# The opening of a gated cross-attention kernel in another order: dense bf16 run, mask as a selection matrix, Wq by column blocks, K and V spread by loads

## The reference, cut to what matters

```
q = (layernorm(x) @ Wq).reshape(B, N, 16, 32)
k = (context @ Wk).reshape(B, 77, 16, 32)
v = (context @ Wv).reshape(B, 77, 16, 32)
scores = where(mask, q . k * 32 ** -0.5, -max)
x = x + tanh(g_xattn) * (softmax(scores) @ v) @ Wo
x = x + tanh(g_ffn) * ffn(layernorm(x))      # fake-quantised gate, up, down; silu(gate) * up
```

## Time and profile before

| | |
|---|---|
| median of three runs | 667.89 us (667.67 to 668.32) |
| the profiled execution, its own time | 665.65 us |
| its span, first to last instruction | 663.9 us |
| PE / VectorE / ScalarE / GpSimd busy | 96% / 76% / 50% / 25% of the span |
| scores of tile 0 begin (slot 0) | 35.3 us after the span's start |

### The profile page before, as it was taken

The page is one execution under the profiler, slowest core; times in us unless marked ns, Lnnn a source line. Parts: engine busy times, 40 slices in busy tenths (PEclk is TensorE's granted clock), DMA queues, the critical chain, the costliest instruction groups (busy, mean ns, idle before and its releaser), DMA issues. The chain is left out here.

```text
span 663.9 us, 12956 instructions
## 1 busy us (share of the span) xinstructions
PE 634.2 (96%) x4035; PEld 479.8 (72%) x4035; DVE 507.3 (76%) x947; ACT 331.9 (50%) x511; POOL 166.5 (25%) x374
## 2 busy tenths in 40 slices
PE   6888999999999999999999997999999999899997
PEld 6578999999999999999999995444444444344443
DVE  4687878878787878877776755799888888866664
ACT  1455454545444554544443442677555554355553
POOL 5122231323232232211110111110111110047775
PEclk9999999999999999999999998999999999999999
DMA  6259311101102010100000001434765110089623
GB/s 224 95 160 305 94 48 25 48 24 40 31 25 47 24 47 24 33 1 1 1 2 1 1 1 41 150 142 81 207 207 197 24 32 17 0 308 395 273 110 117
DMA packets 49687, 59.83 MB, mean 90 GB/s; under 512 B 32084, under 2 KB 32238, under 8 KB 49646
## 3 DMA queue, kind: packets, MB, share of 16 engines
q1 hardware_dynamic: 43854, 42.52, 21.4%
q10 hardware_dynamic: 5792, 16.80, 7.1%
HBM read 32.50 MB, written 19.92 MB: 79 GB/s over the span
## 5 line engine op out<-in xcount | busy, mean ns | idle before, releaser
L523 DVE TENSOR_REDUCE sb_smax<-ps_s 128x8 f32<-128x616 f32 x64 | 51.1, 798 | 64.1 <-PE ps_s L760 63.9
L1161 PE MATMUL ps_g<-sb_xqT,sb_wgu 128*128 128x512 bf16 x352 | 90.3, 379 | 0.6 <-DVE sb_xqT L1129 0.5
L1161 PE MATMUL ps_u<-sb_xqT,sb_wgu 128*128 128x512 bf16 x352 | 90.3, 379 | 0.0
L1046 ACT ACTIVATE sb_silu<-ps_g,sb_sgu 128x512 f32<-128x512 f32 x88 | 60.5, 687 | 59.1 <-PE ps_g L1161 31.9
L429 ACT COPY sb_pT<-ps_p 128x512 f32<-128x512 f32 (+1 forms) x96 | 46.4, 521 | 70.1 <-PE ps_p L771 70.1
L721 PE MATMUL ps_q<-sb_xT_hi,sb_wq_hi 128*128 128x256 f32 x256 | 77.6, 303 | 2.0 <-DVE sb_q_lo L514 1.5
L782 PE MATMUL ps_o<-sb_vblk,sb_pT 128*128 (+4 forms) x640 | 79.0, 270 | 0.1
L1332 PE MATMUL ps_z<-sb_wdT,sb_hq 128*128 128x512 bf16 x352 | 76.1, 379 | 1.2 <-ACT sb_hq L1259 1.2
L782 PEld LDWEIGHTS ps_o<-sb_vblk,sb_pT 128*128 128x128 f32 (+1 forms) x640 | 76.8, 191 | 0.6 <-ACT sb_pT L429 0.3
L1118 DVE SCALAR_TENSOR_TENSOR sb_h<-ps_u,sb_sgu,sb_silu 128x512 f32<-128x512 f32 (+1 forms) x88 | 65.9, 749 | 14.8 <-PE ps_u L1161 13.7
L723 PE MATMUL ps_q<-sb_xT_hi,sb_wq_lo 128*128 128x256 f32 x256 | 72.3, 282 | 0.0
(11 more groups left out here) (156 smaller groups left out, 1350.3 us busy)
## 6 DMA issues: line engine op xcount, KB each, us to landing
h_spill<-sb_h SPq DMA_DIRECT2D x4, 2816.0 KB, 9.5
sb_h<-h_spill ACTq DMA_DIRECT2D x16, 704.0 KB, 6.2
out_dram<-sb_wgu SPq DMA_DIRECT2D x32, 256.0 KB, 2.0
sb_x<-in_x_dram ACTq DMA_DIRECT2D x1, 4096.0 KB, 17.8
sb_w_in<-in_L_ffn_w_gate_dram SPq DMA_DIRECT2D x11, 256.0 KB, 2.7
sb_w_in<-in_L_ffn_w_up_dram SPq DMA_DIRECT2D x11, 256.0 KB, 2.6
sb_h<-in_L_ffn_w_down_dram SPq DMA_DIRECT2D x4, 704.0 KB, 5.9
sb_x<-in_x_dram SPq DMA_DIRECT2D x2, 1024.0 KB, 12.2
```

The source lines that it names most:

```text
L523: dve.tensor_reduce(smax[:, half, :].rearrange("p (g h) -> p g h", g=2), half_scores(), X, ALU.max).then_inc(v_max, 1)
L1046: act.activation(silu[(j * KI + i) % 2][:, :, :].rearrange("p t n -> p (t n)"), p_g[(j * KI + i) % 2][:, :], ACT.Silu, scale=sgu[:, i:i + ...
L1161: last = pe.matmul(banks[(j * KI + i) % 2][:, :], wgu[:, what, k, i * P:(i + 1) * P], xqT[j][:, k, :], start=(k == 0), stop=(k == KD - 1))
```

## The change

The result stays the same function. Loads: `x` tiles 0 and 1 now go first, tiles 2 and 3 ahead of `Wk` and `Wq`, and tiles 8 to 11 come right behind tiles 4 to 7. The mask and the four scalars are loaded to one partition and spread by a product with a row of ones. The masked context is no longer worked out elementwise: VectorE builds a small matrix `pickw` (77 x 77 for each batch), and TensorE multiplies the context by it. The 24 float32 products of the identity become nine bf16 products of 512 columns at the start and two more ahead of the keys. `Wq` is split into high and low parts in four column blocks, each with a wait of its own. The keys leave PSUM by one copy (`kc_hi`) and one subtraction (`kc_lo`), and eight loads on SyncE spread them over `k_hi` and `k_lo`. The values of batch 0 are spread as before but alone; those of batch 1 are made in slot 0 and spread by two groups of six loads between the loads of the feed-forward weights. `wo_hi` moves from slot 1 to slot 0, `wo_lo` from slot 2 to slot 1.

```diff
...
+kc_hi, kc_lo = [spare[:, (5 + 4 * i) * B * M:(9 + 4 * i) * B * M].bitcast(F32R)
+                .rearrange("p (b g m) -> p b g m", b=B, g=KD) for i in range(2)]
+small = spare[:, 13 * B * M:]
 rank, none = small[:, 0:B], small[:, B:2 * B]
-keepT = small[0:M, 2 * B:3 * B]
-c_0 = small[:, 3 * B:(3 + KC) * B].rearrange("p (k b) -> p k b", k=KC)
-mask_u = small[:, P:2 * P].bitcast(U8)[:, 0:B * M].rearrange("p (b m) -> p b m", b=B)
-maskT_u = small[0:M, 2 * P:3 * P].bitcast(U8)[:, 0:B]
-v_sb = pT[0:M, :, :].rearrange("p a n -> p (a n)")[:, 0:B * H * VW]\
-    .rearrange("p (b h d) -> p b h d", b=B, h=H)
+keepT, firstT, rankT, kept = [small[0:M, (2 + i) * B:(3 + i) * B] for i in range(4)]
+rampT_i, rampT = small[:, 6 * B:6 * B + 1].bitcast(I32), small[:, 6 * B + 1:6 * B + 2]
+gate_row = small[0:1, 8 * B:8 * B + 4]
+ones_row = small[0:1, P:2 * P]
+mask_row = small[0:1, 2 * P:2 * P + B * M]
+mask_u = small[0:1, 4 * P:5 * P].bitcast(U8)[:, 0:B * M]
+assert H * VW <= 5 * B * M
+v_sb = [a[0:M, 0:H * VW].rearrange("p (h d) -> p h d", h=H)
+        for a in (pT[:, :, :].rearrange("p a n -> p (a n)"), spare)]
...
+    sp.dma_start(x1[:, 0:2, :], x_v[:, 0:2, :]).then_inc(l_x[0], 16)
     sp.dma_start(c_sb, ctx_in.rearrange("b m c -> m b c")).then_inc(l_ctx, 16)
-    sp.dma_start(x1[:, 0:2, :], x_v[:, 0:2, :]).then_inc(l_x[0], 16)
+    sp.dma_start(x1[:, 2:4, :], x_v[:, 2:4, :]).then_inc(l_x[1], 16)
     sp.dma_start(wk_raw, weights(Wk)).then_inc(l_wk, 16)
     sp.dma_start(wq_raw, weights(Wq)).then_inc(l_wq, 16)
-    sp.dma_start(x1[:, 2:4, :], x_v[:, 2:4, :]).then_inc(l_x[1], 16)
     sp.dma_start(wv_raw, weights(Wv)).then_inc(l_wv, 16)
     sp.dma_start(x1[:, 4:8, :], x_v[:, 4:8, :]).then_inc(l_x[2], 16)
+    sp.dma_start(x1[:, 8:12, :], x_v[:, 8:12, :]).then_inc(l_x[3], 16)
     rows(0)
...
-    sp.wait_ge(v_v, 2 * B)
-    sp.wait_ge(g_zero, 9)
-    for k in range(KB):
-        head0, head1 = heads_of(k)
-        for h in range(head0, head1 + 1):
+    sp.wait_ge(g_zero, 8)
+    for kc, k_blk, done in ((kc_hi, k_hi, a_khi), (kc_lo, k_lo, v_klo)):
+        sp.wait_ge(done, 1)
+        for j in range(HG):
+            rows_j = slice(HD * j, HD * j + HD)
+            sp.dma_start(k_blk[rows_j, :, :, M * j:M * j + M].bitcast(F32).rearrange("p b g m -> p (b g) m"),
+                         kc[rows_j, :, :, :].bitcast(F32).rearrange("p b g m -> p (b g) m")).then_inc(l_k, 16)
+
+    spread = [(k, h) for k in range(KB) for h in range(heads_of(k)[0], heads_of(k)[1] + 1)]
+
+    def values_spread(b, part):
+        sp.wait_ge(v_v, 2 * b + 2)
+        for k, h in part:
             r0, r1 = max(P * k, M * h), min(P * k + P, M * h + M, HW)
-            sp.dma_start(vblk[r0 - P * k:r1 - P * k, :, :, SLOT0[k] + h - head0, :],
-                         v_sb[r0 - M * h:r1 - M * h, :, h:H:HH, :]).then_inc(l_v, 16)
+            sp.dma_start(vblk[r0 - P * k:r1 - P * k, b, :, SLOT0[k] + h - heads_of(k)[0], :],
+                         v_sb[b][r0 - M * h:r1 - M * h, h:H:HH, :]).then_inc(l_v[b], 16)
+
+    sp.dma_start(wo_raw, weights(Wo)).then_inc(l_wo, 16)
+    values_spread(0, spread)
     rows(1)
-    sp.dma_start(wo_raw, weights(Wo)).then_inc(l_wo, 16)
-    sp.dma_start(x1[:, 8:12, :], x_v[:, 8:12, :]).then_inc(l_x[3], 16)
-    rows_transposed(0)
     for w in range(2, NW):
+        rows_transposed(w - 2)
         rows(w)
-        rows_transposed(w - 1)
+        if w in (2, 3):
+            values_spread(1, spread[(w - 2) * len(spread) // 2:(w - 1) * len(spread) // 2])
+        if w == KI:
+            sp.wait_ge(l_k, 16 * 2 * HG)
+            sp.wait_ge(l_v[1], 16 * SLOT0[KB])
+    rows_transposed(NW - 2)
...
-    pool.memset(eps[:, :], EPS).then_inc(g_zero, 1)
     pool.memset(minus[:, :], -1.0).then_inc(g_zero, 1)
     pool.memset(step[:, :], 1.0 / QMAX).then_inc(g_zero, 1)
+    pool.wait_ge(g_ramp, 3)
+    pool.tensor_copy(ramp[:, :, :], ramp_i[:, :, :]).then_inc(g_ramp, 1)
+    pool.tensor_copy(rampT, rampT_i).then_inc(g_ramp, 1)
     pool.memset(k_hi[:, :, :, :].bitcast(F32), 0.0).then_inc(g_zero, 1)
+    pool.wait_ge(g_zero, 6)
+    for n in range(4):
+        deviation(n, n)
     pool.memset(k_lo[:, :, :, :].bitcast(F32), 0.0).then_inc(g_zero, 1)
     pool.memset(vblk[:, :, :, :, :], 0.0).then_inc(g_zero, 1)
-    pool.wait_ge(g_zero, 9)
-    for n in range(5):
-        deviation(n, n)
+    deviation(4, 4)
...
-        if isinstance(n, int) and n == 1:
+        if isinstance(n, int) and n == 0:
             act.wait_ge(l_wo, 16)
             act.copy(wo_hi[:, :, :], wo_raw).then_inc(a_wo, 1)
-
+        if isinstance(n, int) and n == 1:
             act.wait_ge(t_v, B)
-            act.wait_ge(v_wq, 1)
+            act.wait_ge(v_wq, KD)
...
-    act.dma_start(mask_u[:, :, :], mask.rearrange("(a b) m -> a b m", a=1)
-                  .broadcast_to([P, B, M])).then_inc(l_mask, 16)
-    for b in range(B):
-        act.dma_start(maskT_u[:, b:b + 1], mask[b:b + 1, :].rearrange("b m -> m b"))\
-           .then_inc(l_maskT, 16)
+    act.dma_start(mask_u, mask.rearrange("(a b) m -> a (b m)", a=1)).then_inc(l_mask, 16)
     for i, a in enumerate((g_xattn, g_ffn, clip_x, clip_down)):
-        act.dma_start(gates[:, i:i + 1], bcast(a)).then_inc(l_small, 16)
+        act.dma_start(gate_row[:, i:i + 1], a.rearrange("(a n) -> a n", a=1)).then_inc(l_small, 16)
+    act.wait_ge(g_zero, 2)
+    act.activation(sg_e[:, 0:1], eps[:, :], ACT.Exp).then_inc(a_dummy, 1)
...
+    def weights_part(g):
+        cols = slice(g * P, (g + 1) * P)
+        act.copy(wq_hi[:, :, cols], wq_raw[:, :, cols]).then_inc(a_wq, 1)
+
     normalise(0, 0)
     x_part(0, 0)
-    normalise(1, 1)
+    act.wait_ge(g_nb, 2)
...
     act.wait_ge(l_wq, 16)
-    act.copy(wq_hi[:, :, :], wq_raw).then_inc(a_wq, 1)
-    x_part(1, 1)
-    act.wait_ge(l_small, 64)
-    act.activation(tg[:, :], gates[:, 0:2], ACT.Tanh).then_inc(a_tg, 1)
-    act.activation(sg_e[:, :], gates[:, 2:4], ACT.Exp, scale=-1.0).then_inc(a_tg, 1)
+    weights_part(0)
+    weights_part(1)
+    x_part(2, 2)
+    weights_part(2)
+    weights_part(3)
     act.wait_ge(t_k, 2)
-    act.wait_ge(g_zero, 7)
-    for j in range(HG):
-        for i in range(2):
-            act.copy(k_hi[HD * j:HD * j + HD, :, 2 * i:2 * i + 2, M * j:M * j + M],
-                     p_k[HD * j:HD * j + HD, i, :, 0:B * M]
-                     .rearrange("p g (b m) -> p b g m", b=B)).then_inc(a_khi, 1)
+    act.copy(kc_hi.rearrange("p b (i g) m -> p i g b m", i=2),
+             p_k[:, :, :, 0:B * M].rearrange("p i g (b m) -> p i g b m", b=B)).then_inc(a_khi, 1)
+    normalise(3, 3)
+    act.wait_ge(t_gate, 1)
+    act.wait_ge(a_dummy, 1)
+    act.activation(tg[:, :], p_gate[:, 0:2], ACT.Tanh).then_inc(a_tg, 1)
+    act.activation(sg_e[:, :], p_gate[:, 2:4], ACT.Exp, scale=-1.0).then_inc(a_tg, 1)
     q_part(0, 0)
-    normalise(2, 2)
-    q_part(1, 1)
-    x_part(2, 2)
-    normalise(3, 3)
     x_part(3, 3)
     normalise(4, 4)
+    q_part(1, 1)
...
+    def values(b):
+        dve.wait_ge(t_v, b + 1)
+        dve.tensor_scalar(v_sb[b][:, :, 0:HD], p_v[b][0:M, :].rearrange("p (h d) -> p h d", h=H),
+                          tg[0:M, 0:1], keepT[:, b:b + 1], ALU.mult, ALU.mult).then_inc(v_v, 1)
+        dve.tensor_copy(v_sb[b][:, :, HD], keepT[:, b:b + 1].broadcast_to([M, H])).then_inc(v_v, 1)
...
+            values(1)
+            dve.wait_ge(v_v, 2 * B)
+            dve.memset(p_p[1][:, 0, :], 0.0).then_inc(v_zero, 1)
...
-        if isinstance(n, int) and n == 2:
+        if isinstance(n, int) and n == 1:
             dve.wait_ge(a_wo, 1)
...
-    dve.wait_ge(t_c, 1)
-    dve.tensor_copy(cT, p_c).then_inc(v_c, 1)
...
-    dve.tensor_tensor(cK, cT, by_chunk(keep), ALU.mult).then_inc(v_mask, 1)
...
-    dve.tensor_tensor(cK, cK, pick, ALU.add).then_inc(v_ck, 1)
...
+    dve.wait_ge(v_mask, 11)
+    for b in range(B):
+        dve.scalar_tensor_tensor(pickw[0:M, b, :], drop[0:M, b, :], firstT[:, b:b + 1],
+                                 pickw[0:M, b, :], ALU.mult, ALU.add).then_inc(v_pick, 1)
+    def query_weights(g):
+        cols = slice(g * P, (g + 1) * P)
+        dve.wait_ge(a_wq, g + 1)
+        dve.tensor_tensor(wq_lo[:, :, cols], wq_raw[:, :, cols], wq_hi[:, :, cols].bitcast(F32),
+                          ALU.subtract).then_inc(v_wq, 1)
...
+    dve.wait_ge(t_ck, 1)
+    dve.tensor_copy(cK, p_ck).then_inc(v_ck, 1)
+    dve.wait_ge(a_xhi, 2)
+    dve.tensor_tensor(xT_lo[0][:, :, P:2 * P], p_x1, xT_hi[0][:, :, P:2 * P].bitcast(F32),
+                      ALU.subtract).then_inc(v_xlo, 1)
+    query_weights(0)
+    query_weights(1)
     x_part(2, 2)
+    query_weights(2)
+    query_weights(3)
+    dve.wait_ge(a_khi, 1)
+    dve.tensor_tensor(kc_lo.rearrange("p b (i g) m -> p i g b m", i=2),
+                      p_k[:, :, :, 0:B * M].rearrange("p i g (b m) -> p i g b m", b=B),
+                      kc_hi.bitcast(F32).rearrange("p b (i g) m -> p i g b m", i=2),
+                      ALU.subtract).then_inc(v_klo, 1)
```

(84 more changed lines are left out.)

123 lines of the change are left out of this document (56 added, 67 removed).

## The result

| | before | after |
|---|---|---|
| median of the runs | 667.75 us (665.30 to 668.58, 10 runs) | 660.32 us (658.60 to 664.70, 10 runs) |
| profiled execution, its own time | 665.65 us | 660.23 us |
| its span | 663.9 us | 658.4 us |
| scores of tile 0 begin | 35.30 us | 26.11 us |

The ratio is 0.9904, 95% interval 0.9883 to 0.9925: faster by some 1%. The forecast was 665.8 us with a range of 663.3 to 669.3 us. In the later comparisons the kernel before had medians of 665.55 to 665.67 us (13 to 29 runs each), against which 660.32 us is 0.8% less: its runs fall in two groups, near 665.5 and near 668 us, and every ratio is taken over such a mix and is not the quotient of the two medians. So beside each ratio I give where a mechanism can be seen without that mix, in the trace.

A forecast was written before the change was run, and what follows sets the result against it. TensorE, busy in 96% of the span, was taken as the bound, with gain only ahead of slot 0: -4.8 us there, +2.7 us in slots 0 to 3, so 667.9 - 2.1 = 665.8 us, range 663.3 to 669.3 us.

The forecast's parts named there:

- Now the same bytes stand ahead of the end of `Wq`: Opening loads: same bytes in another order, so `Wq` lands at 17.4 us and `Wk` at 14 us.
- loads come sooner: Rival, opening: without hundreds of tiny packets `Wq` lands 1.3 us earlier, giving 664.5 us; chance 0.15.
- The keys therefore start at some 14.4 us, as before: Opening: the landing of `Wk` covers the new mask path and dense run, which cost nothing.
- PE's line from the first block: Opening: from `Wq`'s first block at 18.5 us, queries, transposes and values take 11.7 us, ending at 30.2 us.
- The line through the key loads: Opening: `kc_hi` at 20.5 us, eight SyncE issues of 1.0 us, landing 2.0 us; PE's wait ends at 30.5 us.
- (a): Slot 0: VectorE scales batch 1's values, less a saved wait for `xT_lo`: net +0.5 us, bounds 0 and 1.1.
- (b): `wo_hi` stands in front of the copies of `pT`: +1.4 us for PE in slot 1, bounds 0 and 1.9.
- (c): Slot 1: `wo_lo` stands ahead of `q_lo` of tile 3 and `xT_lo` of tile 5: +1.9 us, bounds 0.8 and 2.3.
- (d): Slot 2: the wait for `wo_lo` goes, -1.1 us.
- late key loads: Rival, opening: key loads wait behind others or cost 1.25 us each; slot 0 at 32.5 us, no gain; chance 0.13.
- The clock rival: Opening: gaps after the dense run leave the keys at half clock, +3.3 us, 669.1 us; chance 0.12.
- SyncE as the bound: Rival, opening: each key load takes 1.97 us to issue; keys there at 38.3 us, total 673.6 us; chance 0.10.

The follow-up runs named there:

- e1_wide: Changed kernel with the seven wide mask and scalar loads of before issued again on ScalarE's queue, into unused space: 668.43 us, ratio to the kernel before 1.0039.
- e6_late: Kernel before with the transposed mask and four scalars issued behind the first normalisation on ScalarE: 668.62 us, ratio 1.0037.
- e13_warm16: Kernel before with 16 identity products ahead of the keys in place of 24: 666.12 us, ratio 0.9995.
- e4_whole: Changed kernel with the first tile's queries waiting for all four column blocks of `Wq`: 661.18 us, ratio to the kernel before 0.9926.
- e3_wo: Changed kernel with `wo_hi` back in slot 1 and `wo_lo` back in slot 2: 658.19 us, ratio to the kernel before 0.9875.
- e12_vlate: `e8_halves` with the values of batch 1 moved behind VectorE's first score work of slot 0: 657.02 us, ratio to the kernel before 0.9860.
- e11_stats: Kernel before with VectorE's statistics of `x` tiles 0 and 1 moved ahead of the rest of the mask's chain: 667.96 us, ratio 1.0024.
- e15_both: `e14_xfirst` with the four scalars' loads issued behind the copies of the keys: 665.36 us, ratio to the kernel before 0.9987.
- e5_nodense: Changed kernel without its eleven dense bf16 products: 666.05 us, ratio to the kernel before 0.9984.
- e14_xfirst: `e11_stats` with TensorE's transpose of `x` tile 0 moved ahead of the keys: 666.33 us, ratio to the kernel before 1.0002.
- e2_order: Changed kernel with its first five loads in the order of before: 666.50 us, ratio to the kernel before 1.0007.
- e7_kcopies: Changed kernel with K put in place by the sixteen copies and subtractions of before, no key loads: 663.01 us, ratio to the kernel before 0.9943.
- e8_halves: `e3_wo` with `wo_lo` made in two halves in slot 2, the first earlier in the slot: 656.61 us, ratio to the kernel before 0.9861.

## Why the prediction was wrong, step by step

**What bounds.** "From the steady slots there is nothing to gain" held: -9.2 us lie ahead of slot 0 and +3.5 us in slots 0 to 3.

**"Now the same bytes stand ahead of the end of `Wq`... so `Wq` lands at 17.4 us, and `Wk`... at 14 us"** is the step that failed. It took the rate of the loads from the kernel before, where it was 90 to 108 GB/s from 2 to 6 us, and never asked for the cause of that rate, though the 1.97 us issue was in hand. `Wq` landed at 13.3 us and `Wk` at 10.6 us; `e1_wide` (`Wq` at 16.9 us) and `e6_late` (12.4 us, where the kernel before had 16.1) show that the small loads on ScalarE's queue made the difference. The rival "loads come sooner" named the mechanism but priced it at 1.3 us, with a chance of 0.15; it measured 4.1 us against the 17.4.

Both landings had to be wrong for the miss. The working had two lines to the queries of tile 0 that ended together: the first block of `Wq` at 18.5 us, and the keys, from 14.4 us, through at 18.3 us. With `Wq` alone sooner the queries would have begun at 18.3. They began at 15.09 us because the keys were sooner too, and it was the end of the keys that let them go, not the block.

**"The keys therefore start at some 14.4 us, as before"** failed by 2.8 us, with the landing of `Wk` that stood under it. What the working said for that case came true: with the cover of `Wk` gone the mask path was the start of the chain (`cK` copied at 11.44 us, keys at 11.61). I had also not asked what held the keys at 14.34 us before. It was neither `Wk` (11.9 us) nor `cK` (12.75 us) but the 24 identity products, by `e13_warm16`.

**PE's line from the first block** was nearly right in length: 11.7 us forecast, 26.11 - 15.09 = 11.0 us measured. It began 3.4 us sooner than the 18.5 us forecast. The block split measured 1.6 us (`e4_whole`, with the reserve made there).

**The line through the key loads.** `kc_hi` was due at 20.5 and was done at 16.57 us. I took 1.0 us per issue; eight took 5.38 us with their gaps, 0.67 each, at the cheap end of my bounds. I took 2.0 us for the landing; it was 4.4 and 3.6 us in the median, 3.6 for the last. The two errors cancel in part: from `kc_hi` to the last landing at 25.04 us it was 8.5 us, where I had 10.0, and PE, at slot 0 from 26.11 us, never waited for the loads. By the Trainium skill (DMA: Bandwidth & Descriptors, Specifications), whose 0.6 us to the first byte I had set beside it, the landing would have been further off still.

**Slots 0 to 3.** (a) +0.5 forecast, +0.9 measured, within its bounds: with `Wo` back in its place (`e3_wo`) the way from slot 0 to the block's end is 392.69 - 26.10 = 366.59 us, where before it was 400.94 - 35.30 = 365.64. The wait for the probabilities grew from 0.7 to 1.7 us, and without these casts (`e12_vlate`) it is 0.7 us again. (b) and (c) as forecast in kind: waits of 1.2 and 1.8 us (+1.4 and +1.9 in the sum); (d) -1.1 as it stood. Together +2.7 forecast, +3.5 measured. Missing was the clock: behind the wait for `q_lo` came a stretch of 3.4 us at half rate, worth about 1.0 us by `e4_whole`. Of (b) to (d), forecast at +2.2 us net, the block's end shows 2.55 us (`e3_wo`).

**Sum.** Forecast -2.1 us, block's end -5.7 us: the opening was off by -4.4 us and the slots by +0.8. The other 1.9 us to the median come from adding 2.2 us for the distance of the profiled execution from the median of before. The later medians of before lie at its profiled time, so that distance was one of its two groups and no property of it. `e11_stats`, with slot 0 0.4 us late and a profiled time of 667.91 us, shows such an execution: the clock stays at half for 13.7 us at the entry of the feed-forward stage in place of 6.8 us, as in `e15_both`. For the slower group of before this is shown in part. No profile fell on it, but each run has its mean granted clock: of the 109 later runs of the kernel before, all 79 up to 666.02 us have 0.991 or more (0.9925 on average), and 22 of the 30 from 667.19 us on have 0.990 or less (0.9895). The other eight overlap with the first group, so the clock is not shown to be all of it.

Two slips of the working changed no step above. SyncE's issue decides the sign from (35.3 - 2.7 - 22.5) / 8 = 1.26 us on, as the rival of late key loads has it; 1.43 us is where the kernel would be 0.2% slower. And sooner loads with (b) and (c) at half their price give 664.5 - 1.65 = 662.9 us, not 663.3; the measured time lies below either.

**The clock rival** did not come in the changed kernel: its first twelve key products took 1.74 us. The dense run covers the keys, and without it they ran twice as long (`e5_nodense`, 3.45 against 1.74 us). That is the rule of the Trainium skill (TensorE: Matmul & The Clock Gate, What's actually happening), half clock until activity releases it, and the trace agrees. Its mechanism did come in `e1_wide`, where PE waited 4.2 us between the dense run and the keys, and in the slots, where a wait was added. **SyncE as the bound** did not come: issues were 0.67 us. **Late key loads** did not come either: the last landed 1.1 us ahead of slot 0.

**What the sum leaves open.** One part at a time undone, slot 0 moves back by 3.4 us (order of loads), 4.2 (dense run), 3.7 (values first), 1.6 (blocks), 0.9 (K) and 7.9 us (wide loads): 21.7 us in all, where the change gave 9.2. (`e1_wide` puts back more than the kernel before had, so its share is rather too large.) One part at a time done in the kernel before gives -0.6 to +2.4 us. The parts are steps of one chain, and no share can be given to one of them. `e15_both` shows three of them together reach -1.84 us, where `e11_stats` alone had +0.4 and `e14_xfirst` -0.5 us.

## What to carry to other kernels

Before a sum takes a transfer's time from the trace, ask what set that time: the DMA share and GB/s of the first stretches and issues of 2 us say that something holds them, and it may be the thing the change removes. When several chains end within a microsecond or two, undoing or doing one of them measures nothing of the whole; list for each the next that would be late, with its time. And look at a station behind the edited stretch, here the end of the attention block, since the clock at a later border can take back or add 2 us without any edit there.

## What the runs showed of the hardware

- Seven loads of nearly 900 small packets, issued in the first 7.5 us, went with 81 to 108 GB/s in stretches that had 285 to 294 GB/s without them, and with single issues on either queue of 1.6 to 2.0 us in place of 0.3 to 0.5 us. With the wide mask alone at the start (`e6_late`) the stretch from 2 to 4 us had 72 GB/s and the next 225; with only the four scalars moved (`e15_both`) it was 95 and 108, so the mask's loads do most of it up to 6 us.
- An issue can also be long without them: in the kernel after the load of `x` tiles 8 to 11, the eighth on SyncE, took 3.50 us to issue. Why was not tested.
- Twelve value loads took 10.3 us to issue (23.27 to 33.57 us) with half the pieces, as long as before (10.4 us): the issue on SyncE did not shrink with them, where I had taken 0.75 us each. A key load of 32 x 8 pieces took 0.67 us.
- At the entry of the feed-forward stage the granted clock was at half for 6.8 us in eight of the profiled executions and for 13.7 us in three, with nothing changed there; the other six (`e2_order`, `e3_wo`, `e5_nodense`, `e7_kcopies`, `e8_halves`, `e12_vlate`) had 3.4 us twice or 6.8 and 3.4 us, with full clock between. What follows the block's end took 262.8 to 263.3 us with 6.8 us at half, 264.8 us with 13.7 (`e11_stats`, `e13_warm16`, `e15_both` within 0.1) and 264.2 to 265.6 us with a split. What decides between them was not settled.
- A wait of 1.75 us for `q_lo`, which left PE 0.25 us busy in 44 to 46 us, was followed by 3.4 us at half clock. It came in every kernel with `wo_lo` in slot 1, between 46 and 58 us, but `e4_whole`, and in none of the three changed kernels with it in slot 2.
